# Layer 1's experts: places of their own for 16 of 19 weight blocks, fetched in a row, in place of two groups of places taken in turn

## What is computed (the reference, cut to what matters)

```python
logits = hidden @ router_w.T
top_vals, top_idx = top_k(logits, 1)
scores = sigmoid(-inf everywhere but top_vals at top_idx)
routed_in = hidden[None] * scores.T[:, :, None]
gate, up = split(einsum('nth,nhf->ntf', routed_in, gate_up_proj), 2)
routed_out = einsum('ntf,nfh->nth', up * silu(gate), down_proj)      # F = 128
shared = silu(hidden @ shared_gate_w.T) * (hidden @ shared_up_w.T) @ shared_down_w.T
return shared + routed_out.sum(0)
```

## Time and profile before

| | |
|---|---|
| median of 3 runs | 2075.65 us (2063.01 to 2077.3) |
| profiled execution, its own time | 2065.72 us |
| its span, first to last instruction | 2063.9 us |
| busy, share of the span | PE 81%, PEld 46%, DVE 65%, ACT 45%, POOL 38% |
| granted TensorE clock, mean | 0.902 |
| fetches of expert weights | 152, 192 KB each (19 for each of 8 blocks) |

### The profile page before, as it was taken

One profiled execution on the slowest core, in us unless ns is written; L12 is line 12 of the kernel. 1 busy time (PEld: TensorE's weight loads), 2 busy tenths in 40 slices (PEclk: granted clock), 3 DMA queues, 4 the chain that ended last, 5 costly groups with the idle time before them and its releaser, 6 DMA issues.

```text
span 2063.9 us, 28747 instructions
## 1 busy us (share of the span) xinstructions
PE 1661.8 (81%) x10612; PEld 957.0 (46%) x10660; DVE 1346.3 (65%) x3057; ACT 921.3 (45%) x1623; POOL 793.0 (38%) x670
## 2 busy tenths in 40 slices
PE   7787698777888778788688877897778896799767
PEld 4455564322545556343155556642135565565114
DVE  4653447998654445797965545578986553458996
ACT  3443234554445323545445433365444552236643
POOL 2320213777241121575813211156761321115882
PEclk9999899987999989899799989998789999699878
DMA  6003311121000341202100044021200024202110
GB/s 203 1 6 110 98 52 49 39 67 31 11 1 1 104 130 31 67 22 67 31 11 1 5 128 117 15 67 37 72 11 6 1 61 142 62 1 72 57 47 11
DMA packets 91982, 105.42 MB, mean 51 GB/s; under 512 B 7104, under 2 KB 70336, under 8 KB 91584
## 3 DMA queue, kind: packets, MB, share of 16 engines
q1 hardware_dynamic: 89792, 99.37, 16.2%
q0 software_dynamic: 2048, 4.20, 0.7%
HBM read 80.60 MB, written 22.94 MB: 50 GB/s over the span
## 4 chain that ended last, share of the span: by engine, by line
PE 48%; DVE 18%; issue 14%; POOL 7%; ACT 5%; SPq 5%; DMA 4%; DVEq 0%; ACTq 0%; POOLq 0%
PE P L229 9%; DVE M L2024 7%; PE P L1641 5%; POOL M L2094 5%; PE P L1870 4%; SPq L1464 3%; SPq L1465 2%; PE P L1224 2%; DMA W<-in_e 2%; PE P L1229 2%; PE P L1240 2%; PE P L2152 1%; PE P L1817 1%; PE P L218 1%; PE P L969 1%
## 5 line engine op out<-in xcount | busy, mean ns | idle before, releaser
L2024 DVE TENSOR_TENSOR_SCAN M<-P,M 128x512 f32<-128x512 f32 x384 | 446.7, 1205 | 16.2 <-ACT P L1951 13.1
L1870 PE MATMUL P<-M,wt 32*32 32x512 f32 x3072 | 256.5, 736 | 125.2 <-DVE M L2024 95.5
L1951 ACT ACTIVATE P<-M,negA 128x512 f32<-128x512 f32 x384 | 263.0, 690 | 207.1 <-DVE M L2024 206.1
L229 PEld LDWEIGHTS P<-wt,M 128*128 128x128 f32 x2176 | 278.2, 194 | 97.2 <-issue 31.6
L229 PE MATMUL P<-wt,M 128*128 128x128 f32 x2176 | 293.4, 281 | 15.2 <-DVE M L1738 3.5
L2094 POOL TENSOR_TENSOR M<-M 128x512 f32<-128x512 f32 x192 | 239.3, 1282 | 134.2 <-DVE M L2009 99.6
L2094 POOL TENSOR_TENSOR M<-W,M 128x512 f32<-128x512 f32 x192 | 242.7, 1297 | 57.9 <-PE P L1870 57.9
L210 POOL TENSOR_TENSOR st<-st,wt 128x4 f32<-128x4 f32 x64 | 83.8, 1310 | 253.4 <-DVE st L193 253.2
L1870 PEld LDWEIGHTS P<-M,wt 32*32 32x32 f32 x3072 | 38.7, 113 | 280.2 <-DVE M L2024 211.4
L1641 PE MATMUL P<-M,wt 128*128 128x512 f32 x256 | 142.3, 639 | 9.6 <-ACT M L1690 4.8
L1738 DVE TENSOR_TENSOR M<-M,P 128x512 f32<-128x512 f32 x128 | 87.2, 683 | 73.8 <-PE P L1649 41.7
(11 more groups left out here) (344 smaller groups left out, 3284.6 us busy)
## 6 DMA issues: line engine op xcount, KB each, us to landing
W<-in_e SPq DMA_DIRECT2D x152, 192.0 KB
M<-dt SPq DMA_DIRECT2D x48, 256.0 KB, 4.7
M<-xs SPq DMA_DIRECT2D x32, 256.0 KB, 4.4
ys<-M SPq DMA_DIRECT2D x32, 256.0 KB, 2.3
W<-du SPq DMA_DIRECT2D x32, 256.0 KB, 4.9
W<-xh SPq DMA_DIRECT2D x16, 256.0 KB
M<-du SPq DMA_DIRECT2D x16, 256.0 KB, 5.0
xs<-zero SPq DMA_DIRECT2D x2, 1216.0 KB, 8.9
```

Of the source, the lines that this page charges most:

```text
L229: m = e.matmul(out[:, tok(j)], h[:, tok(j)], wgt, start=first and j == 0, stop=last, skip_group_check=True)
L1870: m = e.matmul(t["sums"][i // 2][to:to + 32, :], part("WC", c)[r, r], scan[r, :], start=c == 0, stop=c == 5, tile_position=(32 * i, to))
L1951: e.activation(t["aa"][n % 2][:, :], t["dtr"][i][:, :], EXP, scale=negA[:, c:c + 1]).then_inc(ACT.s, ACT.mark(b, "a3", "aa", n))
L2024: e.tensor_tensor_scan(bb[:, :], t["aa"][n % 2][:, :], bb[:, :], 0.0, MUL, ADD).then_inc(DVE.s, DVE.mark(b, "a3", "scan", n))
```

## The change

`f1_weights` now gives a block's weights one of 16 places: the eight of `W`, five in tiles 22 to 25, two in tiles 19 and 20, one in tile 1. Blocks 16 to 18 (group 4) take the first three places of `W` again, once down(0) has read them. There is a semaphore for each group in place of two. SyncE's order in one f1 becomes: wait for `eb`; fetch(0); wait for `tokens_out`; sorted tokens of group 0; fetch(1); sorted tokens 1 and 2; fetch(2); sorted tokens 3 and 4; fetch(3); wait for `y(0)`, its store; wait for down(0); fetch(4); then wait and store for y(1) to y(4). What TensorE, VectorE, ScalarE and GpSimd do in f1 is the same, in steps of the same number. All five lists of `TURNS` are written anew, over the whole run and not in f1 alone: the lengths stay, the order of the two lanes' steps differs. The lists are cut here.

```diff
--- before.py
+++ after.py
@@ -130,7 +130,7 @@
         tokens_out = [sem(f"tokens_out{s}") for s in range(2)]
         tokens_back = [sem(f"tokens_back{s}") for s in range(2)]
         sorted_in = [[sem(f"sorted_in{s}_{g}") for g in range(-(-NBLK // 4))] for s in range(2)]
-        experts_in = [[sem(f"experts_in{s}_{i}") for i in range(2)] for s in range(2)]
+        experts_in = [[sem(f"experts_in{s}_{g}") for g in range(-(-NBLK // 4))] for s in range(2)]
 
         dt_d, du_d, xh_d = ([nc.dram_tensor(f"{n}{s}", [128, T], f32, kind="Internal").ap() for s in range(2)]
                             for n in ("dt", "du", "xh"))
@@ -1168,13 +1168,14 @@
 
         GROUPS = [range(4 * g, min(4 * g + 4, NBLK)) for g in range(-(-NBLK // 4))]
 
-        def f1_turn(b, g):
-
-            return len(GROUPS) * (b // 2) + g
-
         def f1_weights(b, g, i):
-            n = 4 * (f1_turn(b, g) % 2) + i
-            return lanes[b % 2].W[:, 384 * n:384 * n + 384]
+
+
+            L, k = lanes[b % 2], (4 * g + i) % 16
+            if k < 8:
+                return L.W[:, 384 * k:384 * k + 384]
+            at = 22 * T + 384 * (k - 8) if k < 13 else 19 * T + 384 * (k - 13) if k < 15 else T
+            return L.M[:, at:at + 384]
 
         def f1_tiles(b):
             L = lanes[b % 2]
@@ -1215,10 +1216,9 @@
                 m.then_inc(PE.s, PE.mark(b, "f1", "xsT", g))
 
             def expert(g):
-                n = f1_turn(b, g)
                 yield
                 w.wait_ge(ACT.s, ACT.of(b, "f1", "xsT", g))
-                w.wait_ge(experts_in[b % 2][n % 2], 16 * experts_count(b, g))
+                w.wait_ge(experts_in[b % 2][g], 16 * len(GROUPS[g]) * (b // 2 + 1))
                 w.wait_ge(DVE.s, DVE.of(b, "f1", "sw", g + 3))
                 for i, k in enumerate(GROUPS[g]):
                     m = e.matmul(P[2][:, tok(i)], f1_weights(b, g, i)[:, 0:128], xsT[g % 2][:, tok(i)], start=True, stop=True)
@@ -1450,43 +1450,45 @@
 
             return (b // 2) * len(GROUPS[g % 2::2]) + g // 2 + 1
 
-        def experts_count(b, g):
-
-            n = f1_turn(b, g)
-            return sum(len(GROUPS[t % len(GROUPS)]) for t in range(n % 2, n + 1, 2))
-
         def sp_ffn1(e, w, b):
             L, sorted_x, xsT, y, back = f1_tiles(b)
 
             def fetch(g):
-                n = f1_turn(b, g)
                 for i, k in enumerate(GROUPS[g]):
                     expert = e.value_load(L.eb[0:1, k:k + 1], min_val=0, max_val=15)
-                    e.dma_start(f1_weights(b, g, i), we_d[bass.ds(expert * 128, 128), :]).then_inc(
-                        experts_in[b % 2][n % 2], 16)
-
-            yield
-            w.wait_ge(DVE.s, DVE.of(b, "f1", "eb"))
-            for g in range(2):
-                fetch(g)
-            yield
-            w.wait_ge(tokens_out[b % 2], 64 * (b // 2 + 1))
-            for g in range(len(GROUPS)):
+                    e.dma_start(f1_weights(b, g, i), we_d[bass.ds(expert * 128, 128), :]).then_inc(experts_in[b % 2][g], 16)
+
+            def fetch_sorted(g):
                 k0, k1 = GROUPS[g][0], GROUPS[g][-1] + 1
                 e.dma_start(sorted_x[:, k0:k1, :],
                             xs_d[b % 2][128 * k0:128 * k1, :].rearrange("(k p) c -> p k c", p=128)).then_inc(
                     sorted_in[b % 2][g], 16)
-            for g in range(len(GROUPS) + 1):
-                if g:
-                    k0, k1 = GROUPS[g - 1][0], GROUPS[g - 1][-1] + 1
+
+            yield
+            w.wait_ge(DVE.s, DVE.of(b, "f1", "eb"))
+            fetch(0)
+            yield
+            w.wait_ge(tokens_out[b % 2], 64 * (b // 2 + 1))
+            fetch_sorted(0)
+            fetch(1)
+            fetch_sorted(1)
+            fetch_sorted(2)
+            yield
+            fetch(2)
+            fetch_sorted(3)
+            fetch_sorted(4)
+            yield
+            fetch(3)
+            for g in range(len(GROUPS)):
+                if g == 1:
                     yield
-                    w.wait_ge(ACT.s, ACT.of(b, "f1", "y", g - 1))
-                    e.dma_start(y_d[b % 2][128 * k0:128 * k1, :].rearrange("(k p) c -> p k c", p=128),
-                                v3(y[(g - 1) % 2][:, 0:128 * (k1 - k0)], k1 - k0)).then_inc(y_out[b % 2][(g - 1) % 2], 16)
-                    if g + 1 < len(GROUPS):
-                        yield
-                        w.wait_ge(PE.s, PE.of(b, "f1", "down", g - 1))
-                        fetch(g + 1)
+                    w.wait_ge(PE.s, PE.of(b, "f1", "down", 0))
+                    fetch(4)
+                k0, k1 = GROUPS[g][0], GROUPS[g][-1] + 1
+                yield
+                w.wait_ge(ACT.s, ACT.of(b, "f1", "y", g))
+                e.dma_start(y_d[b % 2][128 * k0:128 * k1, :].rearrange("(k p) c -> p k c", p=128),
+                            v3(y[g % 2][:, 0:128 * (k1 - k0)], k1 - k0)).then_inc(y_out[b % 2][g % 2], 16)
 
 
 
@@ -2250,29 +2252,29 @@
@@ -2250,29 +2252,29 @@
         TURNS = {
             "tensor": (2211,
-                "000200f2102106f6fc366ffffa0fe10000002243217e18e1ffe2e5ec61fa378fc5ff087a1e02e003900000079e07bf859993"
...
+                "000000000107abfe1fa7effff50fe100000048b081efff17c68ffc45d2c2101effc30f25f866dd0000003cf0c2015f859996"
...
             "sync": (191,
-                "400ffc003ffcc027fc003ffcc027fc003ffc8127f8007ffa"),
+                "400ffc003ffcc00ffc003ffcc00ffc003ffc8097f8007ffa"),
         }
```

More of the change, by code:

```diff
@@ L2252, in program @@
             "tensor": (2211,
-                "000200f2102106f6fc366ffffa0fe10000002243217e18e1ffe2e5ec61fa378fc5ff087a1e02e003900000079e07bf859993"
-                "fddddddf06fdd0f93ba00f82b0a857ff879a01e51079be4003daffe4d3f7fffa87f0800001089840f7cfd71f0ffe22f68978"
-                "7e1c6ffe01e0f01b000000f3c00006fe14927d0703ddddb7fbbbb003d855e130b7ffffff0f488078db480060d5ff93a5fffd"
-                "b0f81e4610000009f0df277bbde3ee86d88787f0f1bffe01e0f01b000000f3c00007be1ac07f777777eeeef787a56ebe023e"
@@ L2257, in program @@
-                "09c2615fff03d50078daa20003daff93a77ffff547f0800001244c03d5ff277f3cede66941e7e1c3e2ff0e1e0f000079e00f"
-                "2003000de16649fddddddfbbde1e93ab3f0197fffff08f8503dfe"),
+                "000000000107abfe1fa7effff50fe100000048b081efff17c68ffc45d2c2101effc30f25f866dd0000003cf0c2015f859996"
+                "ff03fbbbbff743d66b40178558491bc260408fd480f1603dbe80fdffffffda1fe14007021620002f803cfe2f7ef3ddbccd14"
+                "0f7fe18792fe136e8000001e74003c5f0a499feeec2b777eef787aa6360f067f85915fc3ca00d95079be4003daffe4d3f7ff"
@@ L2259, in program @@
+                "fa87f20000001121c0f793dd9ef3e2e799a48078dff84392fc336e800000003cf007a1ed067f777777ff9dee87adba0027c1"
+                "ac24a5e16ffa0036b079be4003daffe4d37ffff547f080000147803cb5fefdfe4e9e67091ed0c30c6ffffe10e003d6800f20"
+                "0f32440017ffc9b249ffe77700187aa69a0ffffffff08fc20f37e"),
             "scalar": (1540,
-                "01085809337633fd8fb000824807b37ebec8fc538f02e70b0d009ffd60411492494009001135fcf7fed7ee962ffffe10e027"
-                "f803de67d9fda7d801089003ff66ff5f448e25f80e70b007e8750214480040029244d207eebfbaaaafffffffff261eaa8003"
@@ L2262, in program @@
-                "de0cffbd589398004253ef6f7bbd911c4bf80e70b007e8768014524925492004237f85cfffbff5bf6962ff0b1eaa8003de1b"
-                "e7f797d8010a4006ff7ceff6c27112fd81ce00fd301f500214924952004229fe2397fffdfffffff1c01ff"),
+                "0000010f3ccfb3fb4fb000849007ff66febd42017a067d96d007f07d604115000c9294010b7ec8ebff6bfba4abffa5942011"
+                "87be173ffbdcf40025cc005c3fafeef7b220bd033f4b6803ec7a81222924004495200413fff7fd6ffffbd6a2fe10e027f803"
+                "de67d9fda7d800412403f79dfafda4026e033ecb6800bf6b002c524925a2800426ff5a0dffd5fee2ad7fd750e027f803de63"
@@ L2264, in program @@
+                "9ffb97d8010a4025feffb9ee4e1025ffe8182db0c5b47d0010aa480000000425fff7fffffffffff1c04ff"),
             "vector": (2287,
[L2265 to L2268, removed]
@@ L2269, in program @@
-                "52dff73d55771682dfff578c0be87bf480fff87c85bf80000001e7f407e7fff5fe6ff030091204003bbf53ffebff39e0140a"
-                "03000beaf3cfd4024b5762125249249a5f4a9002aa89bffe73f5fffffff86d5501ffe07e"),
+                "0000003fc38a02dfe00000051bf6006f3ffedef9bf8130301020400fc3f53ffffb415886056280c0deaf7817d4037fc49200"
+                "18a492b4beaa802b48b3aaadeab415fff55505bd0c901fffff002dff83e14ff8000000d9fe3b7fff955f063f8100c003a8f5"
+                "5faffffed056219418a0302fabce8de821ffc0552000c124926ac755401e7eaab755fffd057fff55502835c83afffff87c85"
@@ L2271, in program @@
+                "bf800000146fd80ee7ffdbdf3fe040a021104083f3f50fffffc0ac218158a0302fa8f3502d5bf5aa32492495134be95201d5"
+                "4035d556faad057ffeaaa0afd335a41efffff87c85bf80000001e7f407e7fff5fe7fbc0c22800002f47ecffaf5fccff40a88"
+                "007f88073a6fa7df8120a5811544800000197d54401ebefffffffffffff06d5501ffe07e"),
             "gpsimd": (618,
```

(6 more changed lines are left out.)

## The result

| | before | after |
|---|---|---|
| median | 2073.25 us (4 runs) | 1985.7 us (4 runs, 1982.16 to 1987.12) |
| ratio | | 0.9582, 95% interval 0.9544 to 0.9621 |
| span of the profiled execution | 2063.9 us | 1980.4 us |

The change makes the kernel 4.2% faster, some 87 us. I had forecast 2028 us with a range from 1990: the sign was right and the gain nearly twice what I summed.

A forecast was written before the change was run, and what follows sets the result against it. TensorE was taken as the bound, held up in f1 by late weights and tokens (72.8 us of waits). Terms -38 - 14 - 15 + 19 = -48 us gave 2018 us, or 2028 off the median; range 1990 to 2072.

The forecast's parts named there:

- all else: Other lane's steps that now fill 13 us gaps in f1 go elsewhere, where TensorE isn't idle; part of 19 us lost.
- The new lists: Whole run: rewritten order moves 807 of lane 0's 1106 TensorE steps; taken as 0, 15 us to either side.
- neighbouring stretches keep their 84%: Outside f1: stretches like 60 to 150 us keep TensorE 84% busy whichever lane leads.
- waits for weights, 51.6: TensorE's gates in f1: up to 4 us of wait remain per f1, 14 us in all; gain 38 us (20 to 51).
- waits for tokens, 21.2: TensorE's turns in f1: sorted loads go out 4 to 6 us earlier; gain 14 us (10 to 21).
- slow clock in gate, up, down, 27: Expert matmuls run at the lower clock after waits, losing 27 us; gain 15 us (5 to 27).
- gate's wait for the copy: Hand-over of turned tokens to gate in f1: 0.69 us at 32 gates, 22 us, 16 more than now.
- More than I sum (about 1995 us): Rival: new lists fit the stream, f1 runs at 84%, token waits go too; 62 to 80 us less; chance 0.20.
- The gain comes to nothing: Rival: stores queue behind weights in f1, holding ScalarE and down(3) up to 40 us; 2060 to 2078 us; chance 0.17.
- Slower: Rival: SyncE needs 1.49 us per weight block, TensorE idles 13 us each f1; about 2115 us; chance 0.09.
- three signs of being wrong: L1304 waits for stores to ys; SyncE over 1.2 us a block; f1 shrinks 50 us and the rest grows as much.

The follow-up runs named there:

- the mixture: Changed kernel with the new turn order only in one stretch of each pair around f1, the old order elsewhere: 1984.53 us, 0.9616 of the kernel before.
- old_lists: Changed kernel with all five old turn lists, so the weight stream alone: 2019.65 us, 0.9732 of the kernel before.
- two_orders: Changed kernel with each weight block ordered as two transfers, same bytes: 2022.18 us, 0.9755 of the kernel before.

## Why the prediction was wrong

**The sum was one for the stream alone, and it came near that partly by luck.** My 48 us (2028) stand against 55 us measured for the stream under the old lists (2019.65). But the errors of its terms have both signs (table below): the first four give 70 us there where I had 51, and all else takes 12 back where I had 3. **The step that failed is "The new lists. [...] No row prices this; I take 0, with 15 us to either side".** They are worth 25 to 31 us with the stream (0.9732 against 0.9611 and 0.9582) and cost 126 without; with 31 us more my sum would have been at 1997, inside my range but still 11 us short. My reason, that the work is the same and neighbouring stretches keep their 84%, looked at the rest of the run. The lists' worth lies around f1 (the mixture has all of it), most likely in how close the groups stand; the row for it was at hand, the 13.0 us round trip beside 3.2 us of work.

Term by term, in us of gain:

| term | forecast | stream, old lists | changed kernel |
|---|---|---|---|
| waits for weights, 51.6 | 38 (20 to 51) | 49.5 | 49.5 |
| waits for tokens, 21.2 | 14 (10 to 21) | 9.2 | 20.4 |
| slow clock in gate, up, down, 27 | 15 (5 to 27) | 12 | 26 |
| gate's wait for the copy | -16 | -0.7 | -7.3 |
| all else (forecast: the other lane's moved steps) | -3 | -12 | -5 |
| span shorter by | 48 | 57.9 | 83.5 |

The difference of the last two columns, 25.6 us, is what the lists give with the stream: 11 in the waits for tokens, 14 in the clock and 7 in all else, less 7 in hand-overs.

The gain on the weight waits ended above what I took because I set SyncE's end (21 us after the first sorted load) against 17 us of bare TensorE work. TensorE doesn't go so fast: in this f1 of the changed kernel its gates are 4.1 to 4.8 us apart where I had 3.2 (with 0.44 us for a turn whose row says 0.60), and gate(4) starts 22.8 us after that load (162.59 to 185.36). On SyncE's side two sizes were wrong and nearly cancel. The orders end after 20.4 us (182.97) and not 16.6, since a block costs 1.10 us and not 0.91; the earlier trace rows had it, as four orders take 3.64 us and eight 8.09, so that four more cost 4.45. And I added 4.9 us of landing from the earlier trace rows, which I had misread. That row is of all loads into the tile W, attn3's among them. The page of the kernel before, its list of transfers (KB each, median us to landing):

```profile
W<-in_e SPq DMA_DIRECT2D x152, 192.0 KB
...
W<-du SPq DMA_DIRECT2D x32, 256.0 KB, 4.9
```

The 4.9 us are those of `du`; for the weights, which share a semaphore between two groups, it tells no landing at all. With a semaphore for each group the kernel after has one:

```profile
W<-in_e SPq DMA_DIRECT2D x88, 192.0 KB, 2.6
...
M<-in_e SPq DMA_DIRECT2D x64, 192.0 KB, 2.9
```

So a weight lands in 2.6 to 2.9 us in the median, and the last weights are there some 23 us after the first sorted load, just as gate(4) wants them. The clock and the tokens came out in full only with the new lists; for the clock, old_lists' gate, up and down add up to 140.0 us. The hand-overs I overpriced by about half, having put 0.69 us on nearly every gate where 20 of 40 wait. The 3 us for all else were too few under either list.

**The rivals.** "More than I sum (about 1995 us)" was the right side with the right ends for the waits, and still 9 us short. It did say that the new lists fit the stream, but it worked that out from the 84% of the neighbouring stretch with the work in f1 held fixed; my range stopped at 1990 on its strength. "The gain comes to nothing" needed late stores. The kernel after, landing of its stores to ys:

```profile
DMA to landing us min/median/max: 2.0/2.3/4.1
```

2.3 us as before, 4.1 at most, and y's copy (L1304) waits for down, not for a store. The Trainium skill's rule ("DMA: Bandwidth & Descriptors", "Queues, rings and completion order") that descriptors of a row are consumed in ring order may hold, but the price of up to 40 us in this rival is not there. Stores ordered within 0.8 us of a weight's order do land later, in 2.6 to 3.6 us (seven that can be told; the y(0) store of 178.75 in 3.2), against 2.0 to 2.3 for most others: up to 1.3 us more, where the rival took up to 4.9, and no wait of ScalarE comes of it. That the weights ahead cause this is likely and not isolated. "Slower" fell with two_orders. Its sum made each block's extra time a wait of TensorE, from 1.22 us on; at 1.45 to 1.54 it should have idled about 100 us on weights, and the profile has 15.5.

**What I had said the profile would show:** the weight waits near 14 (2.1), the token waits near 7 (0.8), the pitch of fetches 4.3 to 5 (5.4 to 6.3), gate, up and down at 137 (126.3), TensorE at 80% or more in f1 (88%). All moved the way I said and all but the pitch further. Of my three signs of being wrong none came in full: L1304 never waits for a store; SyncE is over 1.2 us for a block (row by number) in three of the forty fetches, 1.35, 1.36 and 1.59, each the first fetch of a block of lane 1; f1 shrank by 115 us and the rest grew by 31.

## What to carry to other kernels

When a change lengthens a look-ahead and rewrites the order of work with it, price the two together: take the round trip that the old order was laid out around, and ask how long the stretch gets once the order no longer has to spread it. A busy share carried over from a neighbouring stretch is a poor bound when work can be moved in and out of the stretch. And an order laid out for a fast supply is dangerous without it: here the same lists are 1.2 to 1.5% better with the stream and 6% worse without. And before a duration goes into a sum, see which transfers its row is of, and whether a merged row of n orders holds n pauses or n-1: two rows of different length give the pitch.

## What the runs showed of the hardware that I had not expected

SyncE starts one of these weight loads every 1.10 us and not every 0.91. The order itself takes 0.33 us; ahead of each lie about 0.77 us, whether the order before was of a weight or of tokens (162.97 to 163.73 and 174.28 to 175.04 in the kernel after). The profile shows in them the read of the expert's number and the arithmetic on it:

```profile
L1458 SPq TENSOR_LOAD <-eb x152: 2/268/713, 156.4 to 1690.1; - x152
L1458 SPq FUSED_REGOPS  x152: 4/152/174, 156.9 to 1690.4; - x152
```

(Durations in ns, min/median/max.) In two_orders the second order of a block, which needs no new number, starts 0.53 us after the first in the median, and the next block's first order 1.10 to 1.12 us after that (starts at 174.54, 175.09, 176.21, 176.73, 177.83 us). So of the 1.10 us of a weight block about half goes into the new number, and an order without one costs 0.53.
